# Three-layer Compressed Interaction Network, one core: five chunks of x lead each of the first two loads, relu writes both halves of the first and last tile's hidden rows, and a few instructions near both ends trade places

## The reference, cut

```python
def _cin(x0, Ws, bs):                    # x0: (512, 32, 64), float32
    h = x0
    for i in range(3):                   # every W has 128 outputs
        Wk = Ws[i].reshape(128, H, 32)   # H is 32, then 64, then 64
        xk = relu(einsum('bhd,bmd,ohm->bod', h, x0, Wk) + bs[i][None, :, None])
        if i != 2:
            outs.append(xk[:, :64]); h = xk[:, 64:]
        else:
            outs.append(xk)
    return concatenate([o.sum(axis=-1) for o in outs], axis=1)      # (512, 256)
```

## Time and profile before

| | us |
|---|---|
| median of 3 runs | 1774.32 (1774.12 to 1774.51) |
| the profiled execution's own time | 1773.69 |
| its span in the trace | 1771.9 |
| busy: PE, DVE, POOL, ACT | 1752.1, 1675.6, 1615.3, 1273.9 |

### The profile page before, as it was taken

How to read it: one execution, slowest core, us unless ns; L and a number is a source line. 1 busy time by engine, 2 the same in 40 slices (tenths; PEclk the granted TensorE clock), 3 DMA queues, 4 the chain that set the end, 5 groups by cost and what they waited for, 6 DMA issues and landing times.

```text
span 1771.9 us, 18843 instructions
## 1 busy us (share of the span) xinstructions
PE 1752.1 (99%) x6676; PEld 1258.4 (71%) x6676; DVE 1675.6 (95%) x915; ACT 1273.9 (72%) x1154; POOL 1615.3 (91%) x387
## 2 busy tenths in 40 slices
PE   7999999999999999999999999999999999999998
PEld 4677777777777777777777777777777777777776
DVE  5999999999999999999999999999999999999996
ACT  4677777777767767777777777677677777776764
POOL 2899999999999999999999999999999999999986
PEclk9899999999999999999999999999999999999999
DMA  6324324334333333244243343332332432433410
GB/s 246 128 88 135 134 80 143 116 98 142 98 117 134 91 131 134 86 137 134 81 143 107 107 141 100 116 134 90 134 134 83 141 130 85 143 110 105 138 33 21
DMA packets 53598, 205.85 MB, mean 116 GB/s; under 512 B 10624, under 2 KB 11648, under 8 KB 45056
## 3 DMA queue, kind: packets, MB, share of 16 engines
q1 hardware_dynamic: 52992, 203.86, 34.8%
q10 hardware_dynamic: 512, 0.79, 0.1%
HBM read 153.75 MB, written 0.52 MB: 87 GB/s over the span
## 4 chain that ended last, share of the span: by engine, by line
PE 96%; DMA 2%; DVE 1%; ACT 1%; issue 0%; POOL 0%; SPq 0%; ACTq 0%; DVEq 0%; POOLq 0%
PE ACC L535 25%; PE ACC L526 25%; PE ACC L528 25%; PE ACC L519 19%; PE ACC L541 3%; DMA X<-in_xrows 1%; DVE ZS L287 1%; DMA H<-H 1%; DVE ZL L303 0%; POOL ZL L383 0%; ACT ZH L426 0%; DVE S L317 0%; ACT H L443 0%; ACT HP L409 0%; ACT WH L458 0%
## 5 line engine op out<-in xcount | busy, mean ns | idle before, releaser
L383 POOL TENSOR_TENSOR ZL<-ZS,ZH 128x2048 fp32r<-128x2048 f32 x382 | 1614.6, 4263 | 147.9 <-ACT ZH L426 147.8
L287 DVE TENSOR_TENSOR ZS<-HP,X 128x2048 f32<-128x2048 f32 x448 | 1011.9, 2282 | 72.3 <-PE ACC L519 60.1
L426 ACT ACTIVATE ZH<-ZS 128x2048 fp32r<-128x2048 f32 x382 | 672.4, 1760 | 18.9 <-DVE ZS L287 18.9
L526 PE MATMUL ACC<-ZH,WL 128*128 128x512 f32 x1664 | 513.9, 427 | 0.9 <-DVE WL L261 0.6
L535 PE MATMUL ACC<-ZL,WH 128*128 128x512 f32 x1664 | 462.9, 397 | 8.4 <-DVE ZL L303 4.7
L409 ACT ACTIVATE HP<-H 128x512 f32<-128x512 f32 x256 | 154.1, 602 | 437.8 <-DVE ZS L287 404.3
L528 PE MATMUL ACC<-ZH,WH 128*128 128x512 f32 x1664 | 460.6, 395 | 0.0
L526 PEld LDWEIGHTS ACC<-ZH,WL 128*128 128x128 f32 x1664 | 313.8, 189 | 128.2 <-issue 48.4
L535 PEld LDWEIGHTS ACC<-ZL,WH 128*128 128x128 f32 x1664 | 312.4, 188 | 86.7 <-DVE ZL L303 6.0
L528 PEld LDWEIGHTS ACC<-ZH,WH 128*128 128x128 f32 x1664 | 312.3, 188 | 76.2
L519 PE MATMUL ACC<-ZS,WF 128*128 128x512 f32 x768 | 351.6, 594 | 0.0
(11 more groups left out here) (34 smaller groups left out, 375.1 us busy)
## 6 DMA issues: line engine op xcount, KB each, us to landing
X<-in_xrows SPq DMA_DIRECT2D x62, 2048.0 KB, 7.5
H<-H SPq DMA_DIRECT2D x252, 128.0 KB, 2.3
XD<-in_xdup SPq DMA_DIRECT2D x64, 256.0 KB, 2.9
H<-H SPq DMA_DIRECT2D x252, 64.0 KB, 2.0
X<-in_xrows SPq DMA_DIRECT2D x4, 1024.0 KB, 8.2
X<-in_w SPq DMA_DIRECT2D x1, 896.0 KB, 10.8
X<-in_w SPq DMA_DIRECT2D x1, 768.0 KB, 15.2
H<-H ACTq DMA_DIRECT2D x4, 128.0 KB, 6.9
```

Of the source, the lines that this page charges most:

```text
L287: nc.vector.tensor_tensor(ZS[:, m % PSLOTS, :, :], h, x, ALU.mult).then_inc(product_ready, 1)
L383: nc.gpsimd.tensor_tensor(ZL[:, n % LSLOTS, c, :], ZS[:, m % PSLOTS, c, :], ZH[:, n % HSLOTS, c, :], ALU.subtract).then_inc(low_by_pool, 1)
L426: nc.scalar.activation(ZH[:, n % HSLOTS, c, :], src, ACT.Copy).then_inc(high_ready, 1)
L526: nc.tensor.matmul(acc, wl[:, k, :], ZH[:, n % HSLOTS, c, :], start=(first and k == 0), stop=False)
```

## The change

It touches the first three stages and the last ones. `HEAD` = 5: the first load of x of tiles 0 and 1 brings five chunks, the second, later in SP's order, three. `direct(t)` holds for tiles 0 and 63: relu writes the hidden rows a second time, to the other half of lay 0, and L179's transfer goes. For tile 0, ACT's copy of lay 0 for layer 1 stands ahead of the issue of the three transfers that are left. `sum12(0)` on DVE and `relu(1, 0)` with the operand copy of tile 2 on ACT stand earlier. The second `keep_warm` has two matmuls and not four. In the last stage DVE's low part of quarter 0 stands ahead of the product of quarter 2.

```diff
--- before.py
+++ after.py
@@ -12,13 +12,14 @@
 BLK = 32
 NB = 128 // BLK
 XC = M // NB
+G = 4
 ROWS = 128 + XC
-G = 4
 Q = 4
 MIXED = 2
 PARTS = {1: 2, 2: 0}
 HEADS = 2
-WARM = 4
+WARM = 4, 2
+HEAD = G + 1
 XSLOTS, PSLOTS, HSLOTS, LSLOTS = 4, 4, 4, 3
 BANKS = 2
 BLOCKS = B // 128
@@ -62,6 +63,16 @@
 
 ORDER = {layer: chunk_order(layer) for layer in (1, 2)}
 NP = {layer: G * (Q - 1) + PARTS[layer] for layer in (1, 2)}
+
+
+def direct(t):
+
+    return t in (0, TILES - 1)
+
+
+def by_dma(t):
+
+    return sum(not direct(k) for k in range(t + 1))
 
 
 def spread_by_act(t):
@@ -152,6 +163,7 @@
         plain_used = sem("plain_used")
         high_ready, high_used = sem("high_ready"), sem("high_used")
         low_by_pool, low_by_dve, low_used = sem("low_by_pool"), sem("low_by_dve"), sem("low_used")
+        direct_done = [sem("direct_done2"), sem("direct_done3")]
         hidden_done = [sem("hidden_done2"), sem("hidden_done3")]
         relu_done = [sem(f"relu_done{n}") for n in range(3)]
         sums12, sums3 = sem("sums12"), sem("sums3")
@@ -176,7 +188,8 @@
             lay0, lay1 = H[layer][:, 0, :], H[layer][:, 1, :]
             src = HID if layer == 0 else 0
             rows = lay0[src:src + HID, :]
-            engine.dma_start(lay0[HID - src:2 * HID - src, :], rows).then_inc(lay0_loaded[layer], 16)
+            if not direct(t):
+                engine.dma_start(lay0[HID - src:2 * HID - src, :], rows).then_inc(lay0_loaded[layer], 16)
             engine.dma_start(lay1[BLK:BLK + HID, :], rows).then_inc(lay1_loaded[layer], 16)
             engine.dma_start(lay1[0:BLK, :], rows[BLK:HID, :]).then_inc(lay1_loaded[layer], 16)
             engine.dma_start(lay1[128 - BLK:128, :], rows[0:BLK, :]).then_inc(lay1_loaded[layer], 16)
@@ -188,10 +201,10 @@
                 to = X[:, t % XSLOTS, :, :].rearrange("p j t -> p (j t)")
                 sp.dma_start(to, src).then_inc(x_loaded[t % XSLOTS], 16)
 
-            def load_x_half(t, half):
-                src = bass.AP(xrows.tensor, (t * ROWS + G * half) * T, [[T, 128], [1, G * T]])
-                to = X[:, t, G * half:G * half + G, :].rearrange("p j t -> p (j t)")
-                sp.dma_start(to, src).then_inc(x_loaded[t] if half else x_head[t], 16)
+            def load_x_part(t, first, end, landed):
+                src = bass.AP(xrows.tensor, (t * ROWS + first) * T, [[T, 128], [1, (end - first) * T]])
+                to = X[:, t, first:end, :].rearrange("p j t -> p (j t)")
+                sp.dma_start(to, src).then_inc(landed, 16)
 
             def load_xd(t):
                 if t >= 1:
@@ -204,16 +217,16 @@
                 sp.dma_start(WF[w + 1][:, :, :], wd[:, n:G * Q, :]).then_inc(wf_loaded[w], 16)
 
             load_xd(0)
-            load_x_half(0, 0)
+            load_x_part(0, 0, HEAD, x_head[0])
             sp.dma_start(W1, w1[:, 0:G, :]).then_inc(w1_loaded, 16)
             sp.dma_start(W1T, w1t).then_inc(w1_loaded, 16)
             sp.dma_start(W5[:, :], w1[:, G, :]).then_inc(w5_loaded, 16)
-            load_x_half(0, 1)
             sp.dma_start(bias_sb[:, :], bias).then_inc(bias_loaded, 16)
             load_xd(1)
-            load_x_half(1, 0)
+            load_x_part(1, 0, HEAD, x_head[1])
             load_weights(0, w2)
-            load_x_half(1, 1)
+            load_x_part(0, HEAD, XC, x_loaded[0])
+            load_x_part(1, HEAD, XC, x_loaded[1])
             load_weights(1, w3)
             sp.dma_start(ident[:, :], ident_in).then_inc(ident_loaded, 16)
             for i in range(TILES + 2):
@@ -269,6 +282,8 @@
                         dve.wait_ge(x_head[i], 16)
                     else:
                         dve.wait_ge(x_loaded[i % XSLOTS], 16 * (i // XSLOTS + 1))
+                if layer == 1 and q == 1 and t < HEADS:
+                    dve.wait_ge(x_loaded[t], 16)
                 p, c = HP[u % BANKS][:, :].ap
                 h = bass.AP(HP[u % BANKS][:, :].tensor, HP[u % BANKS][:, :].offset, [list(p), [0, G], list(c)])
                 x = X[:, t % XSLOTS, G * (q % 2):G * (q % 2) + G, :]
@@ -288,8 +303,6 @@
 
             def narrow(i):
                 u = USE_NO[i, 0, 0]
-                if i < HEADS:
-                    dve.wait_ge(x_loaded[i], 16)
                 if i >= 1:
                     dve.wait_ge(narrow_used, i)
                 nc.vector.tensor_tensor(ZN[:, :], HP[u % BANKS][:, :], X[:, i % XSLOTS, G, :],
@@ -339,6 +352,7 @@
                         sum_w1()
                     narrow(i)
                 if i == 1:
+                    sum12(0)
                     low_w1()
                 if i == 2:
                     low_weights(1)
@@ -350,7 +364,7 @@
                     if i == 1:
                         low(i, 1, 0)
                     product(i, 1, 2)
-                if 0 <= i - 1 <= TILES:
+                if 1 <= i - 1 <= TILES:
                     sum12(i - 1)
                 if live(i - 1):
                     if i > 1:
@@ -359,10 +373,13 @@
                 if live(i - 2):
                     product(i, 2, 0)
                     product(i, 2, 1)
+                    if i == TILES + 1:
+                        low(i, 2, 0)
                     product(i, 2, 2)
                     if live(i - 3):
                         sum3(i - 3)
-                    low(i, 2, 0)
+                    if i <= TILES:
+                        low(i, 2, 0)
                     product(i, 2, 3)
             for n in range(BLOCKS - 1):
                 gather12(n)
@@ -399,8 +416,10 @@
                     act.wait_ge(xd_loaded, 16 * (t + 1))
                     src = XD[:, :]
                 else:
-                    if lay == 0:
-                        act.wait_ge(lay0_loaded[layer - 1], 16 * (t + 1))
+                    if lay == 0 and direct(t):
+                        act.wait_ge(direct_done[layer - 1], t + 1 - by_dma(t))
+                    elif lay == 0:
+                        act.wait_ge(lay0_loaded[layer - 1], 16 * by_dma(t))
                     else:
                         act.wait_ge(lay1_loaded[layer - 1], 48 * (t + 1))
                     src = H[layer - 1][:, lay, :]
@@ -442,6 +461,11 @@
                     act.wait_ge(operand_copied, USE_NO[t + layer, layer + 1, 1] + 1)
                 nc.scalar.activation(H[layer][hid, 0, :], acc[hid, :], ACT.Relu,
                                      bias=b[hid, :]).then_inc(hidden_done[layer], 1)
+                if direct(t):
+                    nc.scalar.activation(H[layer][rest, 0, :], acc[hid, :], ACT.Relu,
+                                         bias=b[hid, :]).then_inc(direct_done[layer], 1)
+                if (t, layer) == (0, 0):
+                    copy_operand(1, 1, 0)
                 if spread_by_act(t):
                     spread_hidden(act, t, layer)
                 if t + layer >= 1:
@@ -467,6 +491,9 @@
                     relu(i - 2, 1)
                 if live(i - 1):
                     high(i, 1, 0)
+                if i == 1:
+                    relu(1, 0)
+                    copy_operand(2, 0, 0)
                 if live(i - 2):
                     copy_operand(i, 2, 0)
                 if live(i - 1):
@@ -486,15 +513,15 @@
                     high_w1()
                     act.wait_ge(bias_loaded, 16)
                     copy_operand(1, 0, 0)
-                if live(i):
+                if live(i) and i != 1:
                     relu(i, 0)
                 if live(i - 2) and i <= TILES:
                     high(i, 2, 0)
-                if live(i + 1) and i >= 1:
+                if live(i + 1) and i >= 2:
                     copy_operand(i + 1, 0, 0)
                 if live(i - 2):
                     high(i, 2, 1)
-                if live(i):
+                if live(i) and i >= 1:
                     copy_operand(i + 1, 1, 0)
                 if i < 2:
                     high_weights(i)
@@ -581,7 +608,7 @@
                     nc.tensor.matmul(acc, R3[:, 0:OUT], R3[:, :], start=True, stop=True)
 
             pe.wait_ge(blank, 1)
-            keep_warm(ACC[0][:, :], WARM)
+            keep_warm(ACC[0][:, :], WARM[0])
             for i in range(TILES + 2):
                 if live(i):
                     layer1(i)
@@ -590,7 +617,7 @@
                         continue
                     acc = wait_bank(i, layer)
                     if i == 1:
-                        keep_warm(acc, WARM)
+                        keep_warm(acc, WARM[1])
                     if i == layer:
                         pe.wait_ge(wf_loaded[layer - 1], 16)
                         pe.wait_ge(w_low, layer)
```

## The result

The changed kernel takes **1768.68 us** (median of 8 runs, 1767.16 to 1769.89) against 1774.02 (median of 8, 1772.87 to 1774.51): ratio 0.9969, 95% interval 0.9959 to 0.998, 5.3 us faster.

The account below looks back on a forecast made before the run. PE, busy in 99% of the span, was taken as the bound, so only its entry into the full stretch and the end count: -2.8 + 0.4 = -2.4 us, predicted 1771.9 us, range 1769.4 to 1773.5.

Parts of the forecast that it names:

- The entry of PE into its full stretch: From 65 to 1735 us PE is always busy, so the start's gain is how much earlier PE enters this stretch.
- the price of tile 0's direct relu: What removing tile 0's two transfers brings: nothing gained at the product to ZP, 2.1 us net behind relu(0, 1).
- the start's -2.8: At the start, POOL's subtraction moves from 55.60 to 52.8, so PE enters its full stretch 2.8 us earlier.
- the first place: Ahead of the product to ZP: a 3.61 us transfer wait goes, a relu with its issues replaces it; 22.4 against 22.23.
- The second place: From relu(0, 1) to POOL, 10.53 us: a 2.12 wait and a 0.63 issue go, a 0.7 relu comes: 8.5.
- The slow first group: PE's first real group, behind a stall of 2.3 us, runs at the lower clock: +1.70 us, bounds 0 and 1.70.
- the forecast's 9.05 us: From the product to ZP to POOL's first subtraction: 8.45 us as before, plus 0.6 for ACT's copy of XD.
- landing at 24: Lay 1's transfers land at 24, ahead of the 25.0 needed, so no cost; landing at 26.6 would cost 1.6 us.
- The issues on ACT: Two relus (1.4), the copy (0.6) and three issues (1.9) stand one behind another on ACT, 3.9 us in all.
- The end: Last layer: 1.1 us gained by the early low part, 1.5 lost to a slow clock behind the new stall: 0.4 slower.
- The rival of the full clock: The clock holds both in the first group and at the end: -4.5 - 1.1 = -5.6, 1768.7 us; 12%.
- The rule of the Trainium skill: Only an idle gap longer than PE's activity-judging time lowers the clock, so none of these stalls would cost anything.

Follow-up runs that it names:

- e1: The changed kernel with its last stage as before (no direct relu for tile 63, low part back in its old place): 1768.44 us, ratio 0.9965.
- e9: The kernel before with only tile 0's second relu at both layers, its transfers gone, and the copy of lay 0 ahead of the issues: 1767.25 us, ratio 0.9959.
- e13: e9 with the second relu for layer 1 of tile 0 alone, all four transfers staying behind relu(0, 1): 1771.78 us, ratio 0.9989.
- e14: e9 with the second relu for layer 2 of tile 0 alone, without the moved copy: 1770.58 us, ratio 0.9983.
- e2: The kernel before with the changed last stage alone (direct relu for tile 63, low part moved): 1774.53 us, ratio 1.0002.
- e7: The changed kernel without the second relu for tile 0, so transfers complete lay 0 again; tile 63 keeps its direct relu: 1774.39 us, ratio 1.0003.
- e8: The changed kernel with the low parts of the layer-3 weights made later on DVE, right ahead of sum12(1): 1767.86 us, ratio 0.9968.
- e10: The changed kernel with e8's edit, the product to ZP ahead of sum12(0), and ACT's first high part ahead of lay 1's copy: 1766.91 us, ratio 0.9952.
- e5: The changed kernel with relu of tile 1 and the copy of tile 2's operand back at their old place on ACT: 1767.61 us, ratio 0.9964.
- e12: The changed kernel run again without any change, for a second profile: 1768.43 us, ratio 0.9966.
- e4: The changed kernel with one dummy matmul at the start instead of four: 1768.5 us, ratio 0.9967.
- e3: The changed kernel with six dummy matmuls at the start instead of four: 1769.0 us, ratio 0.9966.
- e11: e10 with six dummy matmuls at the start and two in the last layer's stall in front of POOL's result: 1763.81 us, ratio 0.9939.

## Why the prediction was wrong

The entry of PE into its full stretch does set the time, and what I named as removed is what was removed. **The step that failed is the price of tile 0's direct relu**, in the start's -2.8: the medians give -5.8 (e1), and the relu alone gives -6.7 (e9). At the first place I let ACT's own row and a slow first group take the place of the removed wait of 3.61 us, so that ZP gained nothing (22.4 for 22.23); alone it measures 2.4 (e13). The second place I priced at 2.1; it measures 3.6 (e14). Beside the forecast's numbers, those of the changed kernel's profile:

| step | forecast | measured |
|---|---|---|
| PE's first group starts, takes | 10.1, 5.40 | 9.97, 3.70 |
| hidden half to R12 on ACT | 3.9 | 3.30 |
| product to ZP | 22.4 | 19.79 |
| POOL's first operation | 31.5 | 30.17 |
| relu(0, 1) | 44.3 | 44.48 |
| from there to POOL | 8.5 | 7.75 |
| PE's last wait for POOL ends | 57.4 | 56.89 |
| start / end / sum | -2.8 / +0.4 / -2.4 | medians: -5.8 (e1) / 0 to +0.3 (e2) / -5.3 |

Between the two profiled executions the forecast's 2.4 us became 5.0: relu(0, 1) came 0.2 late, from there to POOL it was 0.7 shorter, behind PE's entry came 0.6 that I had put at nothing, and the end was 1.5 shorter, the clock that stayed up. That relu(0, 1) came at 44.48 for 44.3 is luck: ZP was 2.6 us earlier than forecast, of which 1.3 went at lay 1's wait and 1.5 in POOL's third operation.

**The slow first group** (the +1.70) is the largest error in front of ZP. It is not certain: e1, e7, e8 and e10 had it, the changed kernel, e5 and e12 not, at the same loads and dummies. And in the changed kernel it is not passed on in full, because ACT copies lay 1 at about 24 in any case: ZP at 19.79 gives POOL at 30.17, 21.51 gives 30.52 (e8), and only from there does POOL follow by the forecast's 9.05 us (22.54 and 31.55 in e4). I had this wait in hand (landing at 24, "no cost") but used it as a bound that is just missed, and not as the cover under which ZP's time matters little. Without the cover the forecast's step holds: e7, e10 and e14 passed the delay on.

**The issues on ACT** are the second error. I added the second relu, the copy and the issues one behind another. The rows show the first issue at 16.00 beside the copy at 15.99, and behind relu(0, 1) the issues beside the second relu (e14: relu at 48.40, its first issue at 48.40): ACT's queue issues a transfer while the engine still works. The issues behind the first are not hidden (ACT is idle for 1.28 us in front of 17.87). That is 0.6 to 0.7 us at each place.

**The first place of the direct relu.** The sum in front of ZP hid its gain: R12's wait takes the transfer's place only if ACT's row is as long as I made it. In e13's trace 1.45 us of it reach relu(0, 1), and 0.7 are left at POOL's next row, where the transfer is still waited for.

**The second place**, 2.1 us forecast with its relu paid for: the rows give 2.8 (7.74 us for 10.53 in e9 and e14), and the rest came behind PE's entry. There, the kernel before had its clock at half from 61 to 65 (0.58 in its profile), and the changed one stood at 1.00 in that stretch and waited 0.75 us for POOL instead (63.82): the last tile's relu moved by 0.6 us more than POOL's start, in the changed kernel as in e14.

**A loss that I did not see** worked against me: POOL's third operation took 6.1 us instead of 4.6, because DVE's subtraction of the layer-3 weights, two tiles in SBUF, came into its time (36.95, 1.80 us). In e1, e4 and e7 it came while POOL's third operation already ran, waited for its end (5.51, 5.25, 5.25), and then held up the fourth (6.1), which comes too late to delay relu(0, 1). Before, it stood at 42.88, when POOL was idle. POOL's subtractions from 28 to 50 in the changed kernel (ns: shortest, median, longest):

```profile
L400 POOL TENSOR_TENSOR ZL<-ZS,ZH x4: 2398/4591/6104, 30.2 to 43.1; 128x2048 fp32r<-128x2048 f32 x3, 128x1024 fp32r<-128x1024 f32 x1
```

The Trainium skill (SBUF — State Buffer, Who interferes with whom) says that a DVE instruction with two SBUF inputs and a GpSimd instruction that reads SBUF block each other for a whole instruction. The trace agrees: POOL's operation of 6.10 us ends at 43.18, 4.4 behind DVE's end at 38.75, and DVE's 5.51 in e1 are the 3.9 us to the end of POOL's operation (41.83) and 1.6 behind it. I had not weighed it, although the diff moves this instruction by several us. Without it the median fell by 0.8 us (e8), with relu(1, 0) at its old place by 1.1 (e5). Both lie inside the spreads, so that these two make up the 1.4 us between e9 and the whole change is likely and not shown.

**The end** agrees with the medians: +0.4 forecast, +0.3 in e2, and 0 to +0.2 between e1 and the changed kernel (1768.43 and 1768.68), all within what can't be told from nothing. Its working was right in one half. The last 30 us take 29.1 at full clock with the old order (e9, e13, e14) as with the new one (the changed kernel, e3, e4), so the 1.1 us that I credited was the clock's loss in the one profile of before. Where the clock falls behind the new stall it is 30.7 (e2: 1772.7 - 1742.0; e5: 1765.8 - 1735.1): 1.6 us, for which I had taken 1.5. It is not certain either: of the ten profiles with the new order four had it (e2, e5, e7, e10), and of the five with the old order two lost 1.1 to 1.2 (the kernel before, e1).

**The rival of the full clock** (1768.7, 12%) gave the measured time to 0.1 us, but not for its reason. Its 4.5 for the start came short by 1.3, its 1.1 for the end isn't there. The rule of the Trainium skill (TensorE: Matmul & The Clock Gate, HAM oscillation) stays refuted as I had put it: the granted clock did fall behind stalls of 2.2 to 2.6 us, in some executions.

**What stays open.** The median gain of the start (5.8) is larger than that between the two profiles (4.0 to 4.6). The profiled execution of before (1773.69) lies 0.3 to 0.6 us below the medians of its runs (1773.96 to 1774.25), and its runs beside the experiments span 1772.39 to 1777.07. Part of this is likely the slow first group, which e7 and e14 pass on with their transfer ahead of ZP, as the kernel before must, and which the changed kernel covers; I have no trace of the kernel before in such an execution. In e9 and e13 the moved copy goes with the second relu, and neither was tried without the other. Which of e10's two reorderings gained what wasn't tried either, nor were e11's dummies on e9.

## What to carry to other kernels

Price a removed wait by doing it alone: here a second relu of 0.7 us at two places, each in place of a transfer that takes about 7 us (6.9 in the earlier trace rows), was the whole gain, and the edits around it added nothing. Before a delay is passed down a chain, list what else is due at the next join; a term costs nothing as far as another wait covers it, and all of the rest, so ask how far the cover reaches and whether the change leaves it standing. When an instruction moves, look at what the other engines do in its new place, DVE beside POOL above all.
